# One-hot matrices of an edge-attention pass made on ScalarE instead of VectorE

## The reference

```python
# pass e0: graph attention, H = 4 heads
alpha = a_src[src_a] + a_dst[dst_a] + a_edge
alpha = jnp.where(alpha > 0, alpha, NEG_SLOPE * alpha)
# pass e21: transformer convolution, H = 8 heads
alpha = jnp.einsum('ehc,ehc->eh', q[dst], k[src]) / np.sqrt(ch)
# both: softmax over the edges that end at one node, then a weighted sum
m = jax.ops.segment_max(alpha, dst, num_segments=n)
ea = jnp.exp(alpha - m[dst])
denom = jax.ops.segment_sum(ea, dst, num_segments=n)
out = jax.ops.segment_sum((ea / denom[dst])[:, :, None] * v[src], dst, num_segments=n)
```

## Time and profile before

| | us |
|---|---|
| median of 3 runs | 4392.54 (4387.63 to 4395.69) |
| the profiled execution | 4394.14, of which the span is 4392.3 |
| busy PE | 2837.4 (65% of the span) |
| busy DVE | 3062.9 (70%) |
| busy ACT | 1079.8 (25%) |
| busy POOL | 2731.0 (62%) |
| line 824, DVE, in e21 (235 instructions) | 147.2 busy, 84.2 idle before them |

### The profile page before, as it was taken

One profiled execution on the slowest core, in us unless ns is written; L12 is line 12 of the kernel. 1 busy time (PEld: TensorE's weight loads), 2 busy tenths in 40 slices (PEclk: granted clock), 3 DMA queues, 4 the chain that ended last, 5 costly groups with the idle time before them and its releaser, 6 DMA issues. The chain is left out here.

```text
span 4392.3 us, 62771 instructions
## 1 busy us (share of the span) xinstructions
PE 2837.4 (65%) x19910; PEld 2520.7 (57%) x19911; DVE 3062.9 (70%) x7097; ACT 1079.8 (25%) x1379; POOL 2731.0 (62%) x2657
## 2 busy tenths in 40 slices
PE   3677676757635656565557466666665657996688
PEld 2566566656635645555556355555555547885566
DVE  4767776777766666676665577777777777997445
ACT  2222232222212222222221212222222223452000
POOL 3777777777557777777771577777777732553000
PEclk7566666656567776767779677776777768998799
DMA  3222222222234445544551233333333314451453
GB/s 71 59 60 60 59 60 59 59 59 60 45 86 126 128 135 140 136 124 132 138 147 50 78 103 102 103 102 103 102 101 102 102 51 98 115 119 32 159 131 90
DMA packets 163300, 415.60 MB, mean 95 GB/s; under 512 B 61300, under 2 KB 88272, under 8 KB 156841
## 3 DMA queue, kind: packets, MB, share of 16 engines
q0 software_dynamic: 95296, 224.30, 19.4%
q1 hardware_dynamic: 64404, 187.52, 16.2%
q10 hardware_dynamic: 3432, 1.61, 0.1%
HBM read 345.77 MB, written 67.48 MB: 94 GB/s over the span
## 5 line engine op out<-in xcount | busy, mean ns | idle before, releaser
L560 POOL DMA_INDIRECT e21G<-table,e21src x858 | 849.4, 990 | 392.0 <-issue 256.8
L560 POOL DMA_INDIRECT e0G<-table,e0src x858 | 858.6, 1001 | 312.1 <-issue 255.4
L1533 POOL DMA_INDIRECT t1G<-table,t1idx x806 | 792.6, 983 | 311.5 <-issue 241.4
L1606 PE MATMUL t1psW<-t1CO,t1G 128*128 128x192 f32 x1612 | 431.6, 430 | 304.4 <-issue 289.1
L1606 PEld LDWEIGHTS t1psW<-t1CO,t1G 128*128 128x128 f32 x1612 | 367.7, 257 | 311.8 <-issue 295.0
L2272 POOL TENSOR_TENSOR e22Z<-e22Z,e22C 121x847 f32<-121x847 f32 (+1 forms) x104 | 200.2, 1956 | 259.6 <-ACT e22Z L2264 259.6
L593 PE MATMUL e0psQ<-Q,e0OT 121*128 x1716 | 307.3, 318 | 39.7 <-issue 35.2
L593 PEld LDWEIGHTS e0psQ<-Q,e0OT 121*128 121x128 f32 x1716 | 305.1, 282 | 45.2 <-issue 45.2
L600 PE MATMUL e21psQ<-Q,e21OT 121*128 x1716 | 246.5, 294 | 102.0 <-DVE e21G L844 62.3
L600 PEld LDWEIGHTS e21psQ<-Q,e21OT 121*128 121x128 f32 x1716 | 214.6, 199 | 134.6 <-DVE e21G L844 89.3
L1845 DVE TENSOR_TENSOR t1AT<-t1AT,t1psW 128x192 f32 x186 | 65.1, 350 | 313.4 <-PE t1psW L1606 312.9
(11 more groups left out here) (445 smaller groups left out, 5766.7 us busy)
## 6 DMA issues: line engine op xcount, KB each, us to landing
e22C<-counts SPq DMA_DIRECT2D x26, 1487.0 KB
llC<-planes SPq DMA_DIRECT2D x52, 743.5 KB
Q<-in_type_p SPq DMA_DIRECT2D x62, 416.0 KB
counts<-X SPq DMA_DIRECT2D x13, 1487.0 KB
planes<-SKIP SPq DMA_DIRECT2D x26, 743.5 KB
counts<-RES SPq DMA_DIRECT2D x13, 1487.0 KB
e0G<-table,e0src POOLq DMA_INDIRECT x858
e21G<-table,e21src POOLq DMA_INDIRECT x858
```

The lines of the kernel that those rows point to most:

```text
L560: nc.gpsimd.indirect_dma_start(out=G[:, u, t, 0:width], out_offset=None, in_=table, in_offset=bass.IndirectOffsetOnAxis(ap=src[:, u, t:t + ...
L1533: nc.gpsimd.indirect_dma_start(out=G[:, q % 2, t, :], out_offset=None, in_=table, in_offset=bass.IndirectOffsetOnAxis(ap=idx[:, q * GT + t ...
L1606: mmi = nc.tensor.matmul(psW[:, k % 2, 0:WIN * NBAS], G[:, q % 2, t, :], CO[:, k % 2, i].rearrange("p b w -> p (b w)"), start=(i == 0), st ...
```

## The change

ACT makes `O` in place of DVE, in the same two operations as `OT`: for each tile t one Square of (2 x iota + place), where `place` is -2 x the edge's local target, one number per partition and tile; then for each batch one Relu of (1 - square). An activation takes one bias per partition, so each tile needs an instruction of its own: 33 squares and 9 relus in a step. The nine comparisons of DVE go. DVE gains one small instruction per step that makes `place`, behind a wait for all nine batches of the previous `O` (`matched`). Each relu waits for its own batch's squares (`gap_squared`). PE's sums wait for `matched` as well as for the values.

Batches 0 to 3 (16 tiles) stand between the big relu of `OT` and the small exponential. Batches 4 to 8 (17 tiles) stand behind the small exponential; at the end of a pair of e0 they stand behind the square roots and ahead of the row stores. `distances` is called where it was.

```diff
+            def match(s, b0, b1):
+                for b in range(b0, b1):
+                    tiles = BATCH[b]
+                    at = slice(tiles[0], tiles[-1] + 1)
+                    act.wait_ge(S["slots_free"], s * NG + (NG + b + 1))
+                    for t in tiles:
+                        m = nc.scalar.activation(O[:, t, :], g["iota"][:, 0:BN], ACT.Square, bias=place[:, t:t + 1], scale=2.0)
+                    m.then_inc(S["gap_squared"], 1)
+                    act.wait_ge(S["gap_squared"], s * NG + (b + 1))
+                    nc.scalar.activation(O[:, at, :], O[:, at, :], ACT.Relu, bias=first_one[:], scale=-1.0).then_inc(S["matched"], 1)
...
                     one_hot(s + 1)
+                    act.wait_ge(S["place_ready"], s + 2)
+                    match(s + 1, 0, 4)
                     act.wait_ge(S["merge_ready"], s + 1)
                     nc.scalar.activation(ex[:], mm[:, 0:2 * H], ACT.Exp).then_inc(S["merge_done"], 1)
+                    if not (gat and u == 1):
+                        match(s + 1, 4, NG)
...
                         nc.scalar.activation(x[:], x[:], ACT.Sqrt).then_inc(S["rooted"], 1)
+                    match(i * 2 + 2, 4, NG)
                     act.wait_ge(S["row_ready"], i + 1)
...
                 V.tensor_scalar(local[:], dst3[:, 1:T + 1], g["base_t"][:, bass.ds(s, 1)], 200.0, ALU.subtract, ALU.min).then_inc(S["local_ready"], 1)
+                if not first:
+                    dve.wait_ge(S["matched"], s * NG)
+                V.tensor_scalar(place[:], dst3[:, 1:T + 1], g["base_t"][:, bass.ds(s, 1)], -2.0, ALU.subtract, ALU.mult).then_inc(S["place_ready"], 1)
...
                     prepare(s + 1, 1 - u)
-                    for b, tiles in enumerate(BATCH):
-                        dve.wait_ge(S["slots_free"], s * NG + (2 * NG + b + 1))
-                        match(tiles[0], tiles[-1] + 1)
                     dve.wait_ge(S["sums_done"], s + 1)
```

## The result

The changed kernel takes 4403.72 us, median of 7 runs (4402.54 to 4407.29); the kernel before takes 4390.94, median of 7 (4385.48 to 4395.69). The ratio is 1.0033, with an interval of 1.0023 to 1.0042. So it is slower, by about 13 us where 40 were forecast.

A forecast was written before the change was run, and what follows sets the result against it. It took e0 as bound by its loop through DVE, PE and ACT, e21 by POOL's gathers. e0 +56.8 and e21 -17 gave +39.8, rounded 40, on 4394.1: 4434, median 4432; range 4393 to 4468, forecast's own 4410 to 4455 (0.64).

The forecast's parts named there:

- e0, start and scores of step 1: Start of e0: shorter first gather (3.5 us) and three shorter gathers of step 1 (0.45 each), -4.9 us.
- e0, 12 boundaries and what else changed in the steps: Ends of e0's pairs: 17 tiles ahead of row stores and table load delay `take_local`; 12 boundaries, +54 us.
- e0, tail: End of e0: the last pair's stores come later behind the root, less 0.5 of acc, +7.7 us.
- e21, relief of POOL: Gathers of e21 no longer lengthened by DVE's comparisons; 1.6 of 1.7 us per pair won, -24 us with the start.
- e21, tail: End of e21: ACT ends at 3601.5 where DVE had ended at 3594.46, +7.0 us.
- stretches without an edit: Program outside e0 and e21: the forecast's sum has no term for it, so 0 us.
- 4.5 us late: Pair's end in e0: first square of `OT` at 300.3 instead of 295.81, delaying spreading, sums and next scores.
- The unrelieved POOL: Rival: long gathers come from writes to `O` or another partner and stay; e21 +7, e0 +61.7, 4461 us; chance 0.08.
- The dear waits: Rival: ACT's batch takes 2.3 us, both halves late, a boundary 7 us; e0 +88, e21 +13, 4494 us; chance 0.10.
- The cheap tiles: Rival: an ACT tile costs 0.20 us, a boundary 1.75; e0 +22, e21 -20, 4394 us, no change; chance 0.12.
- The room at the pair's end: Rival: squares run beside e0's row stores, so boundaries cost nothing; e0 -8, e21 -22, 4363 us; chance 0.06.
- `place`'s wait: DVE at e0's pair end: waits for the last relu, copy of the ends slips 2.9 us, hidden behind ACT's 5.2.

The follow-up runs named there:

- the kernel with the stores first: The changed kernel, with the two row stores of a pair of e0 ahead of ACT's 17 tiles instead of behind them; 4451.56 us, ratio 1.0148.
- the multiplying kernel: The kernel before the change, with a multiplication in place of DVE's comparison in e21, same operands, e0 unchanged; 4391.41 us, ratio 1.0.

## Why the prediction came out as it did

**The forecast was 4432; 4404 was measured.** That is within the stated range of 4393 to 4468, but below the forecast's own range of 4410 to 4455. The direction was right, and the mechanism too: the boundaries of e0 decide, through ACT's queue, and e21 gives back part. The size was about three times too large. By terms, of profiled executions (e0 is cut where the sums of step 1 and those of the last step start, e21's tail at the last small exponential):

| term | predicted | measured |
|---|---|---|
| e0, start and scores of step 1 | -4.9 | -5.4 |
| e0, 12 boundaries and what else changed in the steps | +54 | +36.5 |
| e0, tail | +7.7 | +5.6 |
| e21, relief of POOL | -24 | -25.4 |
| e21, tail | +7.0 | +6.7 |
| stretches without an edit | 0 | -8.5 |
| sum | +39.8 | +9.5 |

**The step that failed is "4.5 us late" for a boundary of e0.** By the spans in the first section a boundary grew by 3.16 us, and 12 of them are 37.9; the rest of the steps became a little shorter, by 1.4 in all. The 1.34 between 4.5 and 3.16 divide so. From the start of the last root to the cast it is 14.04 us, where 299.4 and a root from 284.5 make 14.9: 0.86 too much. Nearly all of it is the tiles: from the root's end the 17 take 8.2 us and not 9.0, since a batch costs 1.88 and not 2.02; what stands behind them took 5.68, and 5.7 was forecast (299.4 less 293.7; the prediction's own 5.85 would have made 299.55, further off). A batch is cheaper mostly because the relu's wait for its own squares is 0.03 us (254.45 against 253.18 + 1.24). I had put 0.12, from the relu of `OT`, whose squares read PSUM and which has a semaphore instruction between its wait and itself; which of the two makes the difference no run shows. The other 0.06 are the four squares, 1.24 and not 1.30. For the same reasons the four batches ahead take 7.6 us and not 8.1, and the small exponential comes 0.8 us earlier behind the sums where I counted 0.4. The stretch from that to the last root is another 0.14 shorter. The other way, cast to square takes 1.03 and not 0.9. These are 0.86 + 0.42 + 0.14 - 0.13 = 1.3, or 16 us in 12 boundaries. An error of 0.1 us a batch isn't much; but it is multiplied by nine batches and twelve boundaries, and what is left of the loss is set against a gain of e21 that is half as large. The largest other part of the miss, 8.5 us, lies in stretches without an edit.

The rule of the Trainium skill that I weighed there ("ScalarE: Activation LUTs", section "What ACT_TABLE_LOAD costs") priced a further tile at 0.29 us, and the trace has 0.29 (four squares in 1.24, one in 0.38, so three further ones in 0.86). Its sum, 3 us lower, was the better one.

**The unedited stretches.** The prediction put them at nothing. 8.5 us of the profile's difference, and about 5 of the medians', are not the change's. The two passes make +18 together, and +12.8 was measured between the medians. One trace can't foretell that part. Of the stretch behind e21 the traces show one thing more: by and large its length goes with the mean granted TensorE clock, from 793 to 794 us at 0.90 of full speed to 803.5 at 0.889.

**e21** went nearly as written: gathers of 0.946 us at the median, but not throughout, since 81 of 858 are still over 0.975, nearly all of them beside other DVE instructions with two inputs in SBUF (line 916, for one); a lag of scores behind the last gather that is 2.8 to 2.9 us in most steps and up to 3.2 in others (once 3.6); and a tail of 6.7. Its end in the kernel after, which answers to the earlier trace rows:

```profile
3598.12 0.22 ACT L671 ACTIVATE e21ex<-e21mm 121x16 f32<-121x16 f32 x1 [0.49 <-DVE e21mm L930]
...
3599.55 0.24 DVE L946 COPY RES<-e21ST 121x145 f32 x1 [0.17 <-issue]
...
3606.15 0.40 ACT L654 ACTIVATE e21O<-e21O,e21first_one 128x121 f32<-128x121 f32 x1
...
3607.67 0.27 DVE L2913 TENSOR_SCALAR f21sm<-RES 121x208 f32<-121x208 f32 x1 [7.88 <-PEq L72]
```

DVE has the pass's result at 3599.79. Until 3606.55 ACT makes one-hots for a step that doesn't exist, and the next phase begins only behind it.

**The rivals.** The unrelieved POOL is refuted by the gathers' means and by the two kernels with an input in PSUM. The dear waits are refuted by the 0.03. The cheap tiles (4394) are nearer to 4404 than the forecast is, but for another reason: a tile costs 0.29 and not 0.20. The room at the pair's end isn't there at that place; it is 12 us earlier, between the roots, and the prediction did not look for it. Of the port: a gather took 4.45 us beside a comparison of 4.26, and 0.94 where one input of the same comparison was in PSUM. By the Trainium skill, "SBUF — State Buffer", section "Who interferes with whom", descriptor generation isn't stalled by a `tensor_tensor`, which the page calls inferred. The trace disagrees in so far as the instruction that issues the gather is held; whether it is held in making descriptors or in reading its row numbers (`e0src`) from SBUF, no run here tells.

**What the prediction got wrong without harm.** It called `place`'s wait, 2.9 us late by its account, hidden behind ACT's 5.2. It was. But it is hidden only as long as ACT is later still: moving `place` was worth 39.68 - 37.09 = 2.6 us a boundary in the kernel with the stores first.

**Open.** Why the stretches without an edit differ by up to 10 us between executions; for the one behind e21 the clock is a candidate, and nothing here separates cause from effect. And what e0 gains beyond its start with `iota` in PSUM.

## What to carry to other kernels

Moved work costs what the queue behind it waits for, at its place: the same 17 tiles cost 55 us more behind the last root than spread behind the small exponential and the first root, where they cost nothing. Look for the idle time of the engine that takes the work, and list what stands behind that place on *every* engine that waits for it, the engine freed included. And if DVE's instructions with two inputs in SBUF run beside indirect DMAs of POOL that bound a pass, put the smaller, repeated input in PSUM: it took 0.8% off this kernel with one added copy in each pass, and DVE's instruction was no slower.

## What the runs showed of the hardware

- An indirect DMA of POOL that is issued beside a DVE `tensor_tensor` with both inputs in SBUF is held when it begins in the midst of it, and ends 0.80 to 0.82 us behind that instruction's end: 4.45 us beside one of 4.26, 1.36 beside one of 0.66, against 0.94 otherwise. In place, and with another operation, it is the same; with either input in PSUM it isn't held. Nor is it when both begin together, to within 0.02 us: then it takes 0.94, and DVE's instruction 0.72 in place of 0.68. A gather that begins behind the end of one, as that of 0.95 at 2944.24 in the rows of the multiplying kernel, isn't held either.
- ACT's activations with an own number per partition, on 128 x 121: 0.38 us alone and 0.29 apart. A relu of 484 columns takes 0.70, and its wait for the squares ahead of it 0.03.
- Squares and relus that stand between exponentials and roots brought no table load: there are 13 ahead of the roots and 26 at `take_local`, before and after.
